# Sixteen token groups of a mixture-of-experts layer: TensorE's program written out instead of looped, and one wait moved

## The reference, cut to what matters

```
q(v)   = fp8 quantise and dequantise with one scale for the whole tensor
x      = x + q(layernorm(x)) @ q(ctx)  + mask          # per batch, 1024x1024x1024
h      = layernorm(x)                                   # 4096 tokens
scores = sigmoid(h @ router_w.T)                        # 32 experts
        # best 3 of 8 groups of experts, then best 4 experts of those; weights normed, times 2.5
        # each expert takes its first C = 160 tokens, in token order
routed = for each expert: (silu(X @ Wg) * (X @ Wu)) @ Wd, times the weight, added to its tokens
shared = (silu(h @ sg.T) * (h @ su.T)) @ sd.T           # inner width 1024
out    = x + routed + shared
```

## Time and profile before

| what | value |
|---|---|
| time, median of 3 runs | 1967.13 us (1966.52 to 1968.06) |
| the profiled execution, its own time | 1967.06 us |
| its span, first to last instruction | 1965.4 us |
| PE busy | 1826.9 us, 93% of the span |
| DVE, ACT, POOL busy | 70%, 44%, 31% |
| mean granted clock of TensorE | 0.995 of full |
| DMA busy in the groups, in the experts | tenths of 2 to 5, and of 9 |

### The profile page before, as it was taken

How to read it: one execution, slowest core, us unless ns; L and a number is a source line. 1 busy time by engine, 2 the same in 40 slices (tenths; PEclk the granted TensorE clock), 3 DMA queues, 4 the chain that set the end, 5 groups by cost and what they waited for, 6 DMA issues and landing times.

```text
span 1965.4 us, 44115 instructions
## 1 busy us (share of the span) xinstructions
PE 1826.9 (93%) x17412; PEld 1398.2 (71%) x17428; DVE 1372.8 (70%) x2509; ACT 864.8 (44%) x1210; POOL 606.4 (31%) x618
## 2 busy tenths in 40 slices
PE   0059999999999999999999999999999999999997
PEld 0037767767866866866776776688888888888886
DVE  5998657457557547656644644588888888888884
ACT  8674212112122222221211211367777777777774
POOL 2200221121122022022022112346556556656652
PEclk9989999999999999999999999999999999999999
DMA  9964552433434344343243255499999999999993
GB/s 379 408 205 106 129 119 69 115 98 83 101 98 96 92 109 94 87 108 98 53 108 97 42 109 169 118 343 350 368 364 349 366 366 354 362 367 347 368 369 87
DMA packets 187634, 395.51 MB, mean 201 GB/s; under 512 B 115377, under 2 KB 119633, under 8 KB 162929
## 3 DMA queue, kind: packets, MB, share of 16 engines
q1 hardware_dynamic: 163264, 334.77, 49.7%
q0 software_dynamic: 23952, 58.81, 13.7%
q10 hardware_dynamic: 288, 0.15, 0.0%
HBM read 314.79 MB, written 55.35 MB: 188 GB/s over the span
## 4 chain that ended last, share of the span: by engine, by line
PE 90%; DVE 2%; issue 1%; DMA 1%; ACT 0%; POOL 0%; POOLq 0%; ACTq 0%
PE ps L1392 54%; PE ps L1405 17%; PE ps L1603 8%; PE ps L1430 5%; PE ps L1611 2%; PE ps L1466 1%; DVE W L1078 1%; PE ps L1525 1%; DMA W<-in_sh_up 1%; PE ps L1471 0%; PE ps L1531 0%; ACT W L729 0%; DVE XT L1113 0%; DVE SG L1247 0%; POOL out_rows L705 0%
## 5 line engine op out<-in xcount | busy, mean ns | idle before, releaser
L1392 PE MATMUL ps<-XT,W 128*128 128x256 f16 (+1 forms) x12192 | 1099.8, 252 | 6.0 <-issue 5.0
L1392 PEld LDWEIGHTS ps<-XT,W 128*128 128x128 f16 x12192 | 1014.3, 98 | 89.3 <-issue 18.5
L1336 DVE SCALAR_TENSOR_TENSOR W<-BIG,W 128x2048 f16<-128x2048 f32 x192 | 436.2, 2286 | 64.5 <-ACT W L901 63.2
L901 ACT ACTIVATE W<-BIG 128x2048 f16<-128x2048 f32 x192 | 361.4, 1901 | 0.0
L1405 PE MATMUL ps<-W,HH 128*128 128x512 f16 x1536 | 334.5, 379 | 0.0
L841 ACT ACTIVATE SG<-ps 128x256 f32<-128x256 f32 x128 | 48.9, 382 | 621.7 <-PE ps L1392 611.6
L1405 PEld LDWEIGHTS ps<-W,HH 128*128 128x128 f16 x1536 | 150.1, 98 | 181.1 <-issue 0.5
L263 POOL TENSOR_TENSOR expo<-expo 128x1 f32<-128x1 f32 x160 | 87.2, 545 | 601.7 <-ACT FR L772 273.9
L1247 DVE SCALAR_TENSOR_TENSOR SG<-ps,SG 128x256 f32<-128x256 f32 x128 | 54.3, 425 | 251.3 <-ACT SG L841 251.3
L578 POOL TENSOR_TENSOR rs<-ve,expo 128x1 f32<-128x1 f32 x32 | 17.6, 551 | 575.9 <-DVE ve L1098 575.9
L632 POOL DMA_INDIRECT FR<-xn_rows,gix x64 | 171.5, 2679 | 30.0 <-issue 30.0
(11 more groups left out here) (192 smaller groups left out, 1629.7 us busy)
## 6 DMA issues: line engine op xcount, KB each, us to landing
BIG<-in_w_gate SPq DMA_DIRECT2D x64, 1024.0 KB, 9.2
BIG<-in_w_up SPq DMA_DIRECT2D x64, 1024.0 KB, 8.8
BIG<-in_w_down SPq DMA_DIRECT2D x64, 1024.0 KB
X<-in_x SPq DMA_DIRECT2D x16, 1024.0 KB, 5.1
X<-in_mask POOLq DMA_DIRECT2D x16, 1024.0 KB, 8.2
xn_rows<-FR SPq DMA_DIRECT2D x32, 512.0 KB
out_rows<-X SPq DMA_DIRECT2D x32, 512.0 KB
W<-in_x SPq DMA_DIRECT2D x6, 2048.0 KB, 22.6
```

The source lines that it names most:

```text
L901: ac.activation(dst, stage, ACT.Copy, scale=W_SCALE).then_inc(x_hi, 1)
L1336: ve.scalar_tensor_tensor(out=lo[cut], in0=src, scalar=W_SCALE, in1=hi[cut], op0=ALU.mult, op1=ALU.subtract).then_inc(x_lo, 1)
L1392: ins = te.matmul(out_ps, a[:, k, cols], b[:, k, :], start=n == 0, stop=n == len(steps) - 1)
```

## The change

TensorE's loop over groups 2 to 9 is gone: all sixteen groups are written out, and each count and address in them is a constant. And the wait for `d_out` at 4 * GROUPS no longer stands ahead of the first expert but ahead of that expert's down product. Nothing is changed in any other engine's program.

```
@@ TensorE's program @@
             pe.wait_ge(rw_lo, 1)
-            group(0, 0)
-            group(1, 1)
-            with pe.Fori(1, 5) as pair:
-                group(pair * 2, 0)
-                group(pair * 2 + 1, 1)
-            for g in range(10, GROUPS):
+            for g in range(GROUPS):
                 group(g, g % 2, front=g < GROUPS - 1)
 
             pe.wait_ge(d_h, 8 * GROUPS)
-            pe.wait_ge(d_out, 4 * GROUPS)
 
             def expert(e, b, more=True):
...
                 pe.wait_ge(x_lo, e * 6 + 6)
                 pe.wait_ge(x_hl, e * 4 + 3)
+                if isinstance(e, int) and e == 0:
+
+                    pe.wait_ge(d_out, 4 * GROUPS)
 
                 wait(pe, x_y, e * 3)
```

## The result

| | time, median (lowest to highest), us | ratio to before, 95% interval |
|---|---|---|
| before, first comparison | 1967.10 (1965.10 to 1968.08), 15 runs | |
| changed | 1962.74 (1961.09 to 1966.99), 15 runs | 0.9981 [0.9974, 0.9988] |
| changed, second comparison | 1960.63, before 1965.62 | 0.9975 [0.9965, 0.9985] |
| changed, third comparison | 1962.31, before 1966.61 | 0.9973 [0.9964, 0.9982] |

It is faster by 4.4, 5.0 and 4.3 us between the medians; 1961.7 was forecast, 5.4 us faster. The profiled execution took 1962.36 us (span 1960.7), 4.70 less than that of before.

The account below looks back on a forecast made before the run. TensorE, busy 93% of the span, was taken to set the time from the groups to the end. Profiled 1967.06 - 4.79 (loop) - 0.65 (wait) = 1961.6 us, as median 1961.7, range 1958.8 to 1964.6.

Parts of the forecast that it names:

- The loop, 4.79 us: TensorE, groups 3 to 10: writing out the loop removes three jumps back and gains 4.79 us, at least 3.55.
- The early transposes: Next group's transposes, issued by SyncE: still there in time when group 4 starts about 1.8 us earlier.
- VectorE's 5.0 us of cover: VectorE at the group border: its own jump back has 5.0 us, where TensorE's took 0.77 to 1.64, so costs nothing.
- the cross products' lateness: TensorE's cross product (L1430), late twice, one in group 3: these 0.9 us go with the loop.
- The moved wait, 0.65 us: TensorE at expert 0: starts 0.83 us earlier, but its down product waits for VectorE's low half, so 0.65 us gained.
- Faster by over 0.2%: Whole kernel: the new median lies under 1963.2 us, 3.9 us being what can be told from no change; chance 0.81.
- A: Group loop: late starts come from another engine's jump and stay; only 0.9 and 0.65 us go, 1965.6 us; chance 0.08.
- B: Expert loop: body fetched anew at 13 jumps back, 1.27 to 2.22 us each, 17 to 29 us, 1985; chance 0.04.
- C: Late in group 15: TensorE's stop at the gate and up products goes too, 2.4 us, 1959.3 us; chance 0.08.

Follow-up runs that it names:

- wait alone: Kernel before with TensorE's loop over groups 2 to 9 kept and only the wait for d_out moved to expert 0's down product: 1964.90 us, ratio 0.9998.
- single loop: Changed kernel with TensorE's groups 2 to 14 as a loop over one group per pass: 1961.94 us, ratio 0.9981 to before.
- six pairs: Changed kernel with TensorE's groups 2 to 13 as a loop of six passes over two groups: 1970.97 us, ratio 1.0019 to before.
- first kernel: Changed kernel with the old wait for d_out put back ahead of the first expert, all sixteen groups written out: 1961.09 us, ratio 0.9978 to before.
- the experiment that forced it: Changed kernel with TensorE's expert loop over four experts per pass, seven passes: 2017.12 us, ratio 1.0248 to before.
- the first four experiments: Second comparison's kernels: groups written out with the old wait 1961.09, wait alone 1964.90, changed kernel again 1960.63, single loop 1961.94 us.

## Why the prediction was right, step by step

**The loop, 4.79 us.** Right in place, cause and size: from group 2 to 10 the trace has 4.70 less, and the other traces put the three jumps at 5.0 (wait alone) and 4.3 (before with the store's wait moved). The early transposes and the other engines' own jumps gave nothing back. One reading behind this was wrong: I held VectorE's 5.0 us of cover against 0.77 to 1.64 us for TensorE's jump, but these are only what is left of it as idle time; the three rows of the jump itself take 4.4 to 5.2 us. Nothing came of it, as VectorE's own jumps take 0.06 us each. That not the jump costs but the body that isn't kept is shown by the single loop (12 jumps, none late) against six pairs (5 jumps, 7.56 us). It was right that the cross products' lateness goes too, but it belongs to groups 3 and 7 and not quite to the loop: 0.04 us are left in each in straight code, 0.32 in the loop over single groups.

**The moved wait, 0.65 us.** The steps held: expert 0 starts at once, the down product meets VectorE's low half and starts 0.10 us behind it. Measured against the store's issue the gain at expert 1 is 21.14 - 20.35 = 0.79 us: the start came 0.99 us earlier and not 0.83, as a start without a wait overlaps the end before it. But it was costed as if nothing but that low half could be late. The step that was missed is ScalarE's wait for the stores: between 3.5 and 5.9 us after the issue, it takes from the gain as soon as it is over 3.96 (21.27 - 17.31) and has taken all at 4.75. Of the nine traces in which TensorE's wait is moved and ScalarE's isn't, five are over 3.96 and three over 4.75. In the time the whole part is 0.5 us (first kernel against the changed one) or 0.7 (the second against before), below what a comparison tells.

**The sum.** 5.44 was forecast and TensorE's last matmuls are 5.44 us earlier, in part by luck, with 4.70 for the loop, 0.70 for what follows (0.79 for the wait, less 0.09 by which group 15 was longer, with more of its stop) and 0.04 from ahead of the groups. The times show 4.3 to 5.0. In the profiled pair the difference is the last scatter's landing, 0.83 us later. For the medians the store's wait may account for some of it (without it the median was 0.9 us under the changed kernel's of that comparison, which is within the spread); the rest is within the spread too. "Faster by over 0.2%", held at 0.81, came out at 0.19%, 0.25% and 0.27% in three comparisons: the gain lies at the bound.

**The rivals.** A (the stops stay) is refuted by the timeline. B (the expert loop is fetched anew) didn't come about, at 21.08 us an expert; the experiment that forced it shows that its price was badly low: 9.2 us a jump and not 1.3 to 2.2. I took the price from a place where 3.9 us of the jump lay beside long matmuls to one where 0.75 did, and left out that so long a stop lowers the clock and that a second stop may follow.

C (the stop in group 15 goes) is refuted as an effect of the change: the stop is in the trace after as before (three late starts, 1.7 us), and is missing in another execution of the same code. It is missing in all four traces of the second comparison (the first four experiments), with TensorE's loop or without, and is there in the ten others. Those four were taken on another chip than the last eight, so it goes with the chip or the occasion and not with this code. Late code isn't it either: in the trace after no code transfer runs between 1243.6 and 1252 us for any engine, while the late starts lie at 1248.8 to 1251.7. I also mis-sized it. Without it TensorE waits 1.0 to 1.2 us for the gathered tokens, so it costs 1.3 us net and not 2.4: group 15 takes 67.86 us with it and 66.55 without. In two traces (experts written out, and the changed kernel for the third time) it costs 2.8, 69.3 us: the 20 matmuls behind the last late start take 4.01 us where 21 take 2.46 in the trace after, at a mean granted clock of 0.56 in the latter of the two. The stop's cause stays open. By its 1.3 us it fits that before was 1.0 to 1.5 us faster in the second comparison than in the others, but there is no trace of before there.

## What to carry to other kernels

Look at what a loop's body holds before blaming its jumps: where TensorE's loop was late at every pass, halving the body cured it as well as writing it out. What a jump out of kept code costs depends on what is beside it: 4 to 5 us in the groups and 5.5 to 6 in the experts, of which the long matmuls of the groups hid 3.9 and left a price of 1.5, and the short ones of the experts hid 0.75, with a lower clock on top, for a price of 9. When a wait is moved off the path, go through every engine that works between its old and its new place, for waits of their own that sat in its shadow; here one on a store, in ScalarE's program, which the list of waits of before shows as idle time behind TensorE. And judge half a microsecond by a timeline, set against an event of the same trace, not by medians.

## What the runs showed of the hardware

TensorE's loop over 1070 instructions (535 matmuls with their weight loads) or 1096 is kept; over 2140 or 2192 it isn't, and nothing between was run. The Trainium skill, page "Runtime: NRT & Kernel Launch", section "Instruction fetch mechanics", gives 2048 for TensorE, and every trace here agrees with that figure. The same section of the Trainium skill says that a taken branch whose target is outside the current 2-page window stalls, with blocks of 256 instructions; by that alone the bodies of 1070 and 1096 would be fetched anew too, and they aren't: in the trace after no code transfer starts between 1406 and 1918 us, while the expert loop runs.

A jump back within a kept body took 0.2 us in TensorE's program, beside matmuls, and cost nothing. Out of the kept code it took 4.2 to 5.2 us at a DMA share of 0.4 to 0.6 during the jump and 5.5 to 6.2 at 0.9 to 1.0; straight code was free at either. The granted clock stayed at 1.00 through the fourteen stops of 0.5 to 1.6 us at the jumps of the groups and was 0.50 around the end of each of the six stops of 5.2 to 5.8 us in the experts. Behind the short stops late in group 15 it fell in two of the ten traces that have them.

A store of 512 KB took 3.5 to 5.9 us from its issue to the instruction behind it, in kernels whose programs for SyncE and ScalarE are the same (3.5, 3.9 and 4.9 in three executions of the changed kernel), and the last scatter 4.3 to 5.6. That alone moves the end by more than this change's second part.
